# Third normalisation's transposes spread over the attention groups of a graph network, with key weights read elsewhere and a new VectorE order

## What is computed

```python
h = relu(layernorm(x)); h = batchnorm(h); h = gcn(h, edges, W_in) + b   # a sum over edges
for i in range(4):
    a = attn(ln(h) * ln2_w + ln2_b, cond, Wq, Wk, Wv, Wo)  # 16 batches of 64 nodes,
    h = h + a                                              # 8 heads of 64, 256 keys each
    u = (ln(h) * ln3_w + ln3_b) @ geglu_w + geglu_b        # 512 -> 4096
    val, gate = split(u)
    h = h + (val * gelu(gate)) @ ffo_w + ffo_b             # 2048 -> 512
return x + gcn(h, edges, W_out) + b + relu(layernorm(x))
```

## Time and profile before

| | |
|---|---|
| median of 3 runs | 2498.57 us (2495.51 to 2499.15) |
| the profiled execution | 2497.86 us, span in the profile 2495.6 us |
| TensorE busy | 2358.2 us, 94% |
| VectorE / ScalarE / POOL busy | 1619.6 (65%) / 1234.7 (49%) / 1061.0 (43%) us |
| mean granted TensorE clock | 0.978 of full |
| chain that ended last | TensorE 69%, VectorE 14%, ScalarE 6%, POOL 4% |

### The profile page before, as it was taken

How to read it: one execution, slowest core, us unless ns; L and a number is a source line. 1 busy time by engine, 2 the same in 40 slices (tenths; PEclk the granted TensorE clock), 3 DMA queues, 4 the chain that set the end, 5 groups by cost and what they waited for, 6 DMA issues and landing times.

```text
span 2495.6 us, 38407 instructions
## 1 busy us (share of the span) xinstructions
PE 2358.2 (94%) x14270; PEld 2065.7 (83%) x14270; DVE 1619.6 (65%) x3031; ACT 1234.7 (49%) x2585; POOL 1061.0 (43%) x726
## 2 busy tenths in 40 slices
PE   7898898899999999999999999999999999899999
PEld 5367888887888999887888999887888999888887
DVE  9975666665656566675556666666556666676554
ACT  9954555653333555653333555654333555553322
POOL 3036666626554222336554322346544322356530
PEclk9998999989999999999999999999999999999999
DMA  2042333302112333202112333212122333212230
GB/s 76 1 165 88 128 143 119 125 28 72 56 55 77 136 119 119 93 26 76 51 55 77 137 117 119 94 35 68 51 72 86 133 114 113 82 51 61 58 124 37
DMA packets 115880, 214.53 MB, mean 86 GB/s; under 512 B 9520, under 2 KB 71600, under 8 KB 113904
## 3 DMA queue, kind: packets, MB, share of 16 engines
q1 hardware_dynamic: 115408, 207.89, 25.0%
q10 hardware_dynamic: 288, 4.19, 0.4%
HBM read 176.13 MB, written 35.91 MB: 85 GB/s over the span
## 4 chain that ended last, share of the span: by engine, by line
PE 69%; DVE 14%; ACT 6%; POOL 4%; issue 4%; DMA 2%; SPq 0%; DVEq 0%; ACTq 0%; POOLq 0%
PE ps L2318 9%; PE ps L2319 8%; PE ps L2320 8%; PE ps L2690 6%; PE ps L2694 6%; PE ps L2692 6%; PE ps L2567 6%; PE ps L2570 6%; PE ps L2569 6%; PE ps L2595 1%; DMA stage<-in_condT 1%; DVE oh_d L1665 1%; PE ps L2891 1%; PE ps L2617 1%; PE ps L2619 1%
## 5 line engine op out<-in xcount | busy, mean ns | idle before, releaser
L2567 PE MATMUL ps<-wv_hi,cb 128*128 128x256 f32 x896 | 258.1, 288 | 17.5 <-ACT kv L1209 7.3
L2567 PE MATMUL ps<-cb,wk_hi 128*128 128x256 f32 x896 | 258.0, 288 | 13.0 <-DVE kv L1968 7.1
L2569 PE MATMUL ps<-cb,wk_hi 128*128 128x256 f32 x896 | 254.0, 283 | 0.0
L2570 PE MATMUL ps<-cb,wk_lo 128*128 128x256 f32 x896 | 254.0, 283 | 0.0
L2569 PE MATMUL ps<-wv_lo,cb 128*128 128x256 f32 x896 | 253.3, 283 | 0.0
L2570 PE MATMUL ps<-wv_hi,cb 128*128 128x256 f32 x896 | 253.3, 283 | 0.0
L813 POOL TENSOR_TENSOR v_lo<-kv,v_hi 128x512 fp32r<-128x512 f32 x96 | 125.7, 1309 | 274.2 <-ACT v_hi L1228 274.0
L853 POOL TENSOR_TENSOR f_lo<-ff,f_hi 128x512 fp32r<-128x512 f32 x128 | 167.8, 1324 | 172.5 <-ACT f_hi L1466 172.5
L2318 PE MATMUL ps<-wf_hi,f_hi 128*128 128x512 f32 x512 | 203.4, 397 | 17.1 <-DVE ff L2233 17.1
L2249 DVE TENSOR_TENSOR h<-h,ps 128x512 f32<-128x512 f32 x256 | 169.5, 683 | 66.1 <-PE ps L2320 65.6
L2319 PE MATMUL ps<-wf_lo,f_hi 128*128 128x512 f32 x512 | 202.6, 396 | 0.0
(11 more groups left out here) (369 smaller groups left out, 6979.8 us busy)
## 6 DMA issues: line engine op xcount, KB each, us to landing
cb<-cb_s SPq DMA_DIRECT2D x168, 512.0 KB, 4.5
stage<-in_pieces SPq DMA_DIRECT2D x256, 128.0 KB, 2.6
cb_s<-cb SPq DMA_DIRECT2D x56, 512.0 KB, 2.6
stage<-in_pieces SPq DMA_DIRECT2D x44, 512.0 KB, 3.6
stage<-in_condT SPq DMA_DIRECT2D x7, 1024.0 KB, 5.5
stage<-in_pieces SPq DMA_DIRECT2D x16, 256.0 KB, 3.3
at_s<-at_hi ACTq DMA_DIRECT2D x2, 2048.0 KB, 12.1
wq_raw<-in_pieces SPq DMA_DIRECT2D x8, 512.0 KB, 7.8
```

What stands on the lines that cost most here:

```text
L2567: pe.matmul(to, l_hi, r_hi, start=(fresh and i == 0 and k == 0), stop=False, skip_group_check=True)
L2569: pe.matmul(to, l_hi, r_lo, start=False, stop=False, skip_group_check=True)
L2570: last = pe.matmul(to, l_lo, r_hi, start=False, stop=(k == 1), skip_group_check=True)
```

## The change

The key weights of the next layer are read, summed and split after MLP products 2 and 4. `t3` is called from group 2 on in each value unit, for tile t-2, always in bank 6; ScalarE's part is cut in two, `x3_full` (the PSUM reads, at the end of each value unit) and `x3_high` (the split, still in the last group), and the first MLP product stands earlier in the last group. In layer 0 the first key weight's sums are made by POOL (`first_sums`, four subtractions and additions as in `attn_sums`) and its splits are placed beside the counting; the query weights are loaded earlier, to a place of their own (`wq_first`). At a layer's start `first_t2(0)` comes one key step earlier, and the second call's fourth transpose goes to the scores' bank, in the order 0, 1, 3, 2 (`T2_ORDER`). VectorE has a new order in both kinds of units. Not shown: `attn_count`, now 48 * (2 * l + 1 + kind), and the indices of the reordered transposes. The diff, cut, with 12 leading blanks taken off:

```diff
-DOWN_PIECE = [2, 6, 10, 13, 16, 19, 22, 25]
-KEY_PIECE, VALUE_PIECE = [5, 9], [26, 27]
+DOWN_PIECE = [2, 5, 8, 12, 15, 19, 22, 25]
+KEY_PIECE, VALUE_PIECE = [11, 18], [26, 27]
...
-T3_BANK = [6, 6, 0, 1, 0, 0, 4, 5]
+T3_BANK = [6, 6, 6, 6, 6, 6, 4, 5]
+KEYS_IN = [2, 4]
...
+load_whole(wq_first, (pieces[2], pieces[3]))
 sp.dma_start(low_s, bits(lo_c0[0:PICKS, :])).then_inc(low_out, 16)
-load_whole(wq_raw, (pieces[2], pieces[3]))
...
-            load_piece(KEY_PIECE[q], 5 + 4 * q)
-        elif q < 2:
-            sp.wait_ge(w_ok, FIRST_PIECES + PIECES * l + KEY_PIECE[q] - 1)
-            load_attn((pieces[base + 13], pieces[base + 17]), q, KEY_PIECE[q] % 2)
+        if q in KEYS_IN:
+            k = KEYS_IN.index(q)
+            if last:
+                load_piece(KEY_PIECE[k], 5 + 4 * k)
+            else:
+                sp.wait_ge(w_ok, FIRST_PIECES + PIECES * l + KEY_PIECE[k] - 1)
+                load_attn((pieces[base + 13], pieces[base + 17]), k, KEY_PIECE[k] % 2)
...
         load_whole(wq_raw, (pieces[base + 5], pieces[base + 9]))
-        load_blocks(0, range(4, BLOCKS), None)
+        load_blocks(0, range(BLOCKS), None)
...
+pool.wait_ge(g_mm, NT)
+pool.wait_ge(xs_lo_ok, NT)
+pool.wait_ge(a_low, 1)
+first_sums()
+pool.wait_ge(a_low, NT + 1)
+attn_low(KEYS, 0, 0)
 for n in range(3):
     cond_sum(0, n)
-attn_low(KEYS, 0, 0)
 attn_low(KEYS, 1, 0)
+for half in range(2):
+    wq_low(0, half)
 cond_low(0, 0)
 cond_sum(0, 3)
-for j in range(1, 4):
-    cond_low(0, j)
+cond_low(0, 1)
 first_rsqrt(0)
 pool.wait_ge(z2_ok, FIRST)
-for j in range(4, BLOCKS):
+for j in range(2, BLOCKS):
     cond_low(0, j)
-for half in range(2):
-    wq_low(0, half)
 for l in range(L):
 
     def first_x2_low(use, k):
...
-    if l == 0:
-        attn_low(VALUES, 0, 0)
     for k in range(2):
         first_x2_low(1, k)
     for n in range(1, 3):
         kv_low(l, 0, KEYS, n)
     if l == 0:
-        attn_low(VALUES, 1, 0)
+        attn_low(VALUES, 0, 0)
+    attn_low(VALUES, 1, l)
+    if l == 0:
...
-        if l == 0 and t < GROUPS - 2:
-            for n in range(2):
-                cond_sum(g + 1, n)
         if not last:
             kv_low(l, t + 1, KEYS, 2)
         if l == 0 and t < GROUPS - 2:
-            cond_sum(g + 1, 2)
+            for n in range(3):
+                cond_sum(g + 1, n)
...
-        for k in range(2):
-            attn_low(VALUES, k, l + 1)
-        first_rsqrt(2 * l + 2)
-        pool.wait_ge(z2_ok, 2 * FIRST * l + 3 * FIRST)
+        attn_low(VALUES, 0, l + 1)
         for half in range(2):
             wq_low(l + 1, half)
+        first_rsqrt(2 * l + 2)
...
+    if f == 0:
+        attn_first()
+    elif f == 1:
+        act.wait_ge(wa_sum, 4)
+        act.activation(attn_place(0, KEYS, 0)[:, 3:7, :], sums_s[:, :, :], ACT.Copy).then_inc(w_hi_ok, 1)
     a_digits(f)
 
-for k in range(2):
-    attn_high(KEYS, k, 0)
+attn_high(KEYS, 1, 0)
+wait_apart(act, picked, 3)
+wq_high(0)
 
...
-wq_high(0)
...
 
+    def x3_full(t):
                                   scale=cols_sb[:, bass.ds(COL["ln3_w"] + KC * l + k, 1)],
                                   bias=cols_sb[:, bass.ds(COL["ln3_b"] + KC * l + k, 1)])
         last.then_inc(full3_ok, 1)
+
+    def x3_high(t):
+
         act.wait_ge(full3_ok, NT * l + t + 1)
         act.activation(xT3_hi[t // 4][:, :, t % 4 * P:(t % 4 + 1) * P],
...
         if last:
             up_high(0)
+            up_high(1)
...
         kv_11_high(t, VALUES)
         pT_high(u)
-        if last:
-            x3_high(0)
         exp_of(u + 1)
...
+            x3_high(0)
         if ahead:
             cond_block(t, 3)
         pT_high(u + 1)
         kv_high(t, VALUES, 2)
         if t:
             o_high(GROUPS * l + t - 1)
+        if last:
+            x3_high(1)
+        elif t > 1:
+            x3_full(t - 2)
 
     def key_units(t):
...
             x3_high(2)
-            x3_high(3)
+            x3_full(5)
...
         else:
+            x3_high(3)
             x3_high(4)
...
-    ahead_high(0)
...
-        if q == 1:
-            ahead_high(1)
+        if q in KEYS_IN:
+            ahead_high(KEYS_IN.index(q))
     wait_apart(act, block_mm, 7 * (short_set(l, MG - 1, 1) + 1))
     if l < L - 1:
-        for k in range(2):
-            attn_high(VALUES, k, l + 1)
+        attn_high(VALUES, 0, l + 1)
         wq_high(l + 1)
+        attn_high(VALUES, 1, l + 1)
...
-attn_sums(KEYS, 0, 0)
-for n in range(2):
+attn_sums(KEYS, 1, 0)
+for n in range(3):
     take_picked(0, n)
-attn_sums(KEYS, 1, 0)
...
         softmax(u)
         kv_two(t, VALUES)
         if t > 1:
             add_bias(t - 2)
         if t:
-            q_low(t, 1)
             o_part(u - 2, 2)
         kv_five(t, VALUES)
         kv_11_low(t, VALUES)
-        pT_low(u)
         maxima(u + 1)
         kv_late(t, VALUES, 0)
         softmax(u + 1)
         kv_late(t, VALUES, 1)
+        pT_low(u)
         if t:
             o_part(u - 1, 3)
+            q_low(t, 1)
         kv_late(t, VALUES, 2)
+        maxima(u + 2)
         pT_low(u + 1)
-        maxima(u + 2)
 
     def key_units(t):
 
...
         if t:
             residual(t - 1, GROUPS * l + t - 1)
         if not last:
             kv_11_low(t + 1, KEYS)
-        pT_low(u)
-        if t:
-            z3_of(t - 1, GROUPS * l + t - 1)
         maxima(u + 1)
-        if last:
-            x3_low(2)
-            x3_low(3)
         if not last:
             kv_late(t + 1, KEYS, 0)
         softmax(u + 1)
         if not last:
             kv_late(t + 1, KEYS, 1)
+        pT_low(u)
+        if t:
+            z3_of(t - 1, GROUPS * l + t - 1)
         o_part(u - 1, 1)
         if last:
+            x3_low(2)
+            x3_low(3)
             o_part(u, 2)
             x3_low(4)
         else:
+            q_low(t + 1, 0)
             kv_late(t + 1, KEYS, 2)
+            maxima(u + 2)
         pT_low(u + 1)
-        if not last:
-            maxima(u + 2)
-        else:
+        if last:
             o_part(u + 1, 3)
             x3_low(5)
             o_low(GROUPS * l + t)
 
     kv_two(0, KEYS)
-    kv_five(0, KEYS)
     for k in range(KC):
...
     first_z2(2 * l + 1, range(FIRST))
     if l == 0:
         attn_sums(VALUES, 0, 0)
-    for k in range(2):
+    for k in T2_ORDER[1][:3]:
         first_x2_full(1, k)
     kv_late(0, KEYS, 1)
-    for k in range(2, KC):
-        first_x2_full(1, k)
...
-    if l < L - 1:
-        attn_sums(KEYS, 0, l + 1)
...
-        if q == 1 and l < L - 1:
-            attn_sums(KEYS, 1, l + 1)
+        if q in KEYS_IN and l < L - 1:
+            attn_sums(KEYS, KEYS_IN.index(q), l + 1)
...
-        if last:
-            t3(0)
+        if t > 1:
+            t3(t - 2)
         p_transpose(u)
         s_product(u + 1, t, 1)
         kv_step(t, VALUES, 4)
         kv_step(t, VALUES, 5)
         if t:
             pv_product(u - 1, t - 1, 3)
-        if last:
-            t3(1)
         kv_step(t, VALUES, 6)
-        if last:
-            t3(2)
         p_transpose(u + 1)
...
         else:
-            t3(3)
+            pe.wait_ge(w_ok, FIRST_PIECES + PIECES * l + 2)
+            pe.wait_ge(x3_ok, 2 + NT * l + 2)
+            pe.wait_ge(full3_ok, NT * l + 6)
+            mlp_product(0, 0, 0, 0, slice(0, 2 * P))
...
         else:
+            mlp_product(0, 0, 0, 1, slice(0, 2 * P))
             pv_product(u, t, 2)
-            t3(4)
-            pe.wait_ge(w_ok, FIRST_PIECES + PIECES * l + 2)
-            pe.wait_ge(x3_ok, 2 + NT * l + 2)
-            mlp_product(0, 0, 0, 0, slice(0, 2 * P))
-            pe.wait_ge(full3_ok, NT * l + 4)
-            mlp_product(0, 0, 0, 1, slice(0, 2 * P))
+            pe.wait_ge(x3_ok, 2 + NT * l + 4)
+            mlp_product(0, 0, 0, 0, slice(2 * P, HALF))
         p_transpose(u + 1)
         if not last:
             s_product(u + 2, t + 1, 0)
         else:
-            t3(5)
-            pe.wait_ge(x3_ok, 2 + NT * l + 4)
-            mlp_product(0, 0, 0, 0, slice(2 * P, HALF))
             pv_product(u + 1, t, 3)
...
     pe.wait_ge(w_ok, attn_piece(KEYS, 1, l) + 1)
-    for j in range(3):
+    for j in range(2):
         kv_step(0, KEYS, j)
     first_t2(0)
-    for j in range(3, 5):
+    for j in range(2, 5):
         kv_step(0, KEYS, j)
     for p in range(3):
         q_product(0, p)
-    first_t2(1, range(2))
+    first_t2(1, T2_ORDER[1][:3])
     q_product(0, 3)
     kv_step(0, KEYS, 5)
-    first_t2(1, range(2, KC))
+    first_t2(1, T2_ORDER[1][3:])
     kv_step(0, KEYS, 6)
     for p in range(PAIRS):
```

More of the change, by code:

```diff
@@ L442, in attn_count @@
                 return 48 * (1 + kind)
-            if attn_piece(kind, k, l) % 2 == 0:
-                return 48 * (2 + l)
-            return 48 * (2 + 3 * (l - 1) + (1, 2, 3)[2 * kind + k if kind == KEYS else 2])
+            return 48 * (2 * l + 1 + kind)
         def raw_block(g, n):
@@ L536, in gnn_preln_kernel, with t2_place, t2_bank @@
         FIRST_BANK = (4, 5, 6, 7)
+        T2_ORDER = (0, 1, 2, 3), (0, 1, 3, 2)
+        def t2_place(use, k):
```

(30 more changed lines are left out.)

61 lines of the change are left out of this document (33 added, 28 removed).

## The result

The changed kernel takes 2527.10 us (median of 4 runs, 2525.96 to 2528.32) against 2498.86 for the kernel before on the same chip (4 runs): ratio 1.0116, 95% interval 1.0098 to 1.0134. It is slower; the forecast was 2484 with a range up to 2511. The profiled execution took 2525.96 us, its span is 2522.8.

The account below looks back on a forecast made before the run. TensorE, busy 94% of the span, was taken as the bound. Terms -23.7 - 5 - 4 + 41.7 + 5.5 - 28.8 = -14.3 us against 2497.9 gave 2483.6, forecast as a 2484 us median, range 2440 to 2511.

Parts of the forecast that it names:

- Part 1: MLPs of layers 0 to 2: moving the key weights removes the ff wait and half-clock work behind it, -23.7 us.
- Part 2: Start of a layer: shorter xT_lo waits, -5 us for layers 1 to 3 and -4 us for layer 0.
- Part 3: Attention groups: late q_low, ScalarE's tile and transposes cost TensorE +41.7 us in layers 1 to 3, +5.5 in layer 0.
- (b): Groups of layers 1 to 3: both q_low halves meet a fresh POOL instruction, +27, so 2511 us; chance 0.17.
- Part 4: Last group of each layer: shorter waits and fewer transposes gain 7.2 us each, -28.8 us for four layers.
- (a): Groups: the new VectorE order costs nothing, as q_low is there in time; total -80, 2418 us; chance 0.17.
- (c): Last groups: wait before wo stays, clock falls each time, -14 in place of -28.8; 2499 us; chance 0.10.
- (d): MLP: the wait moves to product 2 or 4 and the key-weight move gives 0; 2508 us; chance 0.06.
- The slow side: The whole kernel: probability 0.26 given to the changed kernel being slower.

Follow-up runs that it names:

- e14: Changed kernel with only the two wq_low rests put back behind z2 on POOL: 2518.67 us, ratio 1.0089.
- e7: e3 with the second call's transposes in the old split, two ahead of q_product(0,3) and two behind: 2431.65 us, ratio 0.9729.
- e3: Changed kernel with q_low at its old VectorE places and the old order at a layer's end on POOL and ScalarE: 2434.89 us, ratio 0.9753.
- e12: Changed kernel with q_low put back to its old place in the key units alone, still late in value units: 2477.50 us, ratio 0.9925.
- e1: Changed kernel with q_low alone put back to its two old places on VectorE: 2445.03 us, ratio 0.9792.
- e11: e9 with pT_low, z3_of and maxima in the old order too: 2434.76 us, ratio 0.9753.
- e6: e3 with x3_full of tiles 0 to 4 moved on ScalarE behind q_high in the key unit: 2429.03 us, ratio 0.9729.
- e8: Changed kernel with the second rest of the output weights on POOL placed behind the last key rest: 2513.82 us, ratio 1.0068.
- e5: Kernel before with q_low alone moved to its new, late places on VectorE: 2514.15 us, ratio 1.0086.
- e9: The edits of e6 and e7 together, both made on e3: 2419.83 us, ratio 0.9697.
- e4: Kernel before with the key weights alone moved to MLP products 2 and 4: 2464.98 us, ratio 0.9875.

## Why the prediction was wrong

**Part 1** (-23.7): right in mechanism, 5.4 too small; -29.1 measured. The price was read against layer 3, which had 1.4 to gain itself (201.3 to 200.0), and so the difference of 7.9 became 9.3.

**Part 2, layers 1 to 3** (-5): the step that failed, 22.6 us of the 41.5. "so the first of the two `xT_lo` waits (2.5 us together) should go and most of the second stay: -1.7 each, bounds 0 and -2.5" has no loss in its bounds, though the change moves POOL's work to a new place. The prediction said that the query weights' lower parts "are made in the MLP's tail" and costed what they leave, not what they meet. They meet two VectorE sums on SBUF: e14 shows 2.9 to 4.5 us a layer. Another 1.5 to 3.2 are the second call's split, by which VectorE's rests meet POOL's (e7 against e3). Both are what the earlier trace rows show, which the prediction used for `q_low` alone. Nor was the gain there: the two waits for `xT_lo` are 1.2 and 1.1 in e7, where they were 2.5 together. **Layer 0** (-4, measured -4.3): the sum right, the parts less so. The first wait fell by 3.6 us (4.7 forecast), the second by 0.5, and a wait of 2.9 for the value weights came where 2 was estimated; the rest of the gain is not in waits.

**Part 3, layers 1 to 3** (+41.7): the mechanism right, at the place and with the number of waits forecast, and 18.3 too small: the term for the late `q_low` in group 0, and the clock behind it, is most of that. For a steady group, forecast and measured: the late `q_low` in the value unit 1.09 and 1.1 (e12 against e1); in the key unit 0.5 net of the `kv` wait, and 1.1 - 0.45 = 0.65 (e12, e11); the tile on ScalarE 0.35 and 32.45 - 31.90 = 0.55 (e1, e6), of which the wait for `oT_lo` is 0.29; the transposes 0.36 and 0.45 (e11 against before). Together 2.3 and 2.7, 2.0 us a layer for five groups. What was missed is group 0: it was given "0.8 for group 0", on the rows of group 6, and lost 3.3; group 1, given 1.6, lost 3.1. In group 0 POOL also makes the output weights' rests, of 2.5 us, and one half of `q_low` waits for such a one. e8 gives it 3.5 us a layer, with the clock. That is rival (b)'s mechanism, at one group of eight; in the others `q_low` met one instruction, as I had it.

**Layer 0** (+5.5, measured +8.2): inside its bounds. That it gains as well as loses is shown: with `q_low` late in the kernel before its groups get 10 us shorter in all (e5), and in the changed kernel the same move costs 17 (e1).

**Part 4** (-28.8, measured -26.4): waits of 1.42, 2.49, 1.57 and 1.41 came for 1.6, 2.85, 1.45 and 1.3. The clock fell after the one of 2.5 in each layer (0.79 over 8 us), which cost 1.6 us by e9, whose last groups took 57.6 with such a fall and 56.0 without; the 1.5 forecast was near it. The 0.6 us a layer that are missing thus lie in what the old last group was said to lose, not in the new waits.

**The rivals.** (a), that the new order costs nothing, had 0.17: out by e1 and e12, though its remark on the earlier maxima was right (e11). (b) came true in group 0 alone of layers 1 to 3. (c) is out: the wait before `wo` stayed and the clock fell each time, as it said, and yet the last groups gained 26.4 us, not 14. (d) is out by e4. The slow side had 0.26, and the range ended 16 us too low. Part 2's bounds excluded a loss: with the measured +5.9 a layer there my own sum would have been 2507, and an upper end 27 above it, as (b) had, would have held the time. The other 18 us of the error are part 3's.

Of the Trainium skill's rule cited in the prediction (SBUF — State Buffer, "Who interferes with whom"), the runs agree with the sentence that such instructions take turns: e8, e14 and e7 each took a pair apart, and VectorE's side went from 3.78 to 1.75, 2.61 to 0.42 and 3.25 to 1.41 us.
